# Next batch's input norm, u projection, convolution and x projection inside the current pass; z gates one chunk at a time between scans

## The reference, cut to what matters

```python
# 1 Mamba: DIN 512, 16 states, conv of 4 taps
xn = layer_norm(x, ln_g, ln_b);  u, z = split(xn @ W_in.T)
u  = silu(conv4(u) + conv_b)                    # causal, per channel
dt_in, B, C = split(u @ W_x.T)                  # 16 + 16 + 16
dt = softplus(dt_in @ W_dt.T + dt_bias)
h  = exp(dt * A) * h + dt * B * u               # scan over 512 tokens, each (channel, state)
y  = (sum_n h * C + u * D) * silu(z);  x = LN(x + (x + y @ W_out.T))
# 2 slots: x are the slots, ctx (64 rows) the inputs; three rounds, each needs the one before
for _ in range(3):
    a = softmax over slots of rmsnorm(x) @ Wq.T @ (Pn @ Wk.T).T;  a = a / (column sum + eps)
    slots = gru_cell(a @ (Pn @ Wv.T), slots)
x = LN(x + slots)
# 3 FFN: relu(x @ W_fc.T)**2 @ W_proj.T, then five spike steps, their count over 5;  x = LN(x + that)
```

## Time and profile before

| what | value |
|---|---|
| median of 3 runs | 1797.66 us (1795.49 to 1797.7) |
| profiled execution, its own time | 1799.8 us |
| span of the profiled execution | 1797.8 us |
| busy, share of the span | PE 76%, DVE 76%, ACT 55%, POOL 50% |
| mean granted TensorE clock | 0.858 |
| chain that ended last, by engine | DVE 36%, PE 35%, ACT 11%, issue 7%, POOL 7%, DMA 2% |

### The profile page before, as it was taken

How to read it: one execution, slowest core, us unless ns; L and a number is a source line. 1 busy time by engine, 2 the same in 40 slices (tenths; PEclk the granted TensorE clock), 3 DMA queues, 4 the chain that set the end, 5 groups by cost and what they waited for, 6 DMA issues and landing times.

```text
span 1797.8 us, 16320 instructions
## 1 busy us (share of the span) xinstructions
PE 1359.0 (76%) x5472; PEld 818.6 (46%) x5472; DVE 1370.9 (76%) x1509; ACT 984.8 (55%) x1519; POOL 896.8 (50%) x459
## 2 busy tenths in 40 slices
PE   5455867777788769886788768887688868977965
PEld 2344444453456335463356345563355434553433
DVE  3898488956888798868888698868888798863142
ACT  3542566538663756638464666727474566633532
POOL 0665067723775176623676076733676065741120
PEclk9565978888899879998799979998799978997988
DMA  5632153206231343206331344205332153300000
GB/s 178 247 130 94 51 210 118 105 26 209 108 119 46 131 153 118 94 26 211 105 117 58 105 148 134 106 23 201 105 117 70 60 188 127 117 13 12 0 7 18
DMA packets 64762, 188.89 MB, mean 105 GB/s; under 512 B 6224, under 2 KB 22480, under 8 KB 64720
## 3 DMA queue, kind: packets, MB, share of 16 engines
q1 hardware_dynamic: 64720, 188.37, 30.3%
HBM read 183.62 MB, written 4.72 MB: 105 GB/s over the span
## 4 chain that ended last, share of the span: by engine, by line
DVE 36%; PE 35%; ACT 11%; issue 7%; POOL 7%; DMA 2%; DVEq 0%; ACTq 0%; POOLq 0%; SPq 0%; another core or an unknown queue 0%
DVE reg_a L1081 19%; DVE pb L1072 9%; PE pc L632 5%; POOL reg_a L444 4%; PE pb L487 4%; PE py L646 4%; PE pb L606 3%; PE pc L624 3%; PE px L550 3%; PE px L528 2%; DVE reg_m L930 2%; DMA x_out<-reg_m 2%; PE pb L588 2%; DVE u L1045 1%; ACT reg_a L876 1%
## 5 line engine op out<-in xcount | busy, mean ns | idle before, releaser
L444 POOL TENSOR_TENSOR reg_a<-reg_a,cb 128x1024 f32<-128x1024 f32 x256 | 607.4, 2379 | 304.4 <-DVE reg_a L1081 304.4
L1081 DVE TENSOR_TENSOR_SCAN reg_a<-reg_a,pb 128x1024 f32<-128x1024 f32 x256 | 584.6, 2284 | 34.9 <-ACT reg_a L876 24.8
L646 PE MATMUL py<-ident,reg_a 128*128 128x128 f32 x2048 | 326.4, 314 | 84.5 <-POOL reg_a L444 84.5
L876 ACT ACTIVATE reg_a<-dt,neg_a 128x511 f32<-128x511 f32 x512 | 331.8, 710 | 102.0 <-DVE reg_a L1081 101.2
L646 PEld LDWEIGHTS py<-ident,reg_a 128*128 128x128 f32 x2048 | 280.2, 163 | 183.2 <-POOL reg_a L444 120.2
L1072 DVE TENSOR_TENSOR pb<-bb,pb 128x1024 f32<-128x1024 f32 x256 | 314.7, 1229 | 30.0 <-ACT reg_y L836 2.6
L624 PE MATMUL pc<-x2T,w_fc 128*128 128x512 f32 x224 | 119.0, 658 | 27.1 <-DVE reg_y L1098 20.2
L550 PE MATMUL px<-hT,whh 128*128 128x512 f32 x288 | 137.6, 614 | 0.4 <-ACT xs L779 0.4
L406 POOL TENSOR_TENSOR xs<-xs,hT 128x1024 f32<-128x1024 f32 x24 | 56.7, 2361 | 162.7 <-ACT xs L787 162.7
L632 PE MATMUL pc<-w_pr,reg_m 128*128 128x256 f32 x448 | 111.3, 399 | 8.0 <-ACT y_sb L799 4.1
L565 PE MATMUL pb<-ex,vw 64*128 64x512 f32 x48 | 41.7, 964 | 85.1 <-DVE px L997 85.1
(11 more groups left out here) (174 smaller groups left out, 2265.7 us busy)
## 6 DMA issues: line engine op xcount, KB each, us to landing
bb<-bc_rows SPq DMA_DIRECT2D x256, 512.0 KB, 3.6
cb<-bc_rows SPq DMA_DIRECT2D x64, 512.0 KB, 6.0
xin<-x_in SPq DMA_DIRECT2D x9, 512.0 KB, 3.6
xs<-x_in SPq DMA_DIRECT2D x8, 512.0 KB, 3.5
x_out<-reg_m SPq DMA_DIRECT2D x8, 512.0 KB, 3.4
w_in<-w_inT_in SPq DMA_DIRECT2D x1, 1024.0 KB, 7.1
w_fc<-w_fcT_in SPq DMA_DIRECT2D x1, 1024.0 KB, 10.9
w_pr<-w_prT_in SPq DMA_DIRECT2D x1, 1024.0 KB, 13.2
```

The source lines that it names most:

```text
L444: pool.tensor_tensor(h[:, g % HR], h[:, g % HR], cb[:, 2 * q:2 * q + 2], ALU.mult).then_inc(s["hc_done"], 1)
L646: mm = pe.matmul(py[:, cols_], h[:, g % HR, j, cols_], ident[:], is_transpose=True, start=(q == 0 and j == 0 and i2 == 0), stop=(q == PAIR ...
L876: ins = act.activation(d_a[:, g % DR, j, 1:], dt[:, c, 1:], ACT.Exp, scale=neg_a[:, c * NS + n + j:c * NS + n + j + 1])
L1081: dve.tensor_tensor_scan(h2[:, g % HR], d_a2[:, g % DR], pb[:, 1:3, :].rearrange("p a t -> p (a t)"), 0.0, ALU.mult, ALU.add).then_inc(s[" ...
```

## The change

Four things, taken together.

- The input norm, u projection, convolution, u gate and x projection of batch i+1 are made in pass i (those of batch 0 in the set-up). Convolution steps read the projection straight from PSUM; `upad`, its zeroing and one of the two copies go. The B and C rows are written to DRAM before the barrier, so a pass begins with the dt projection, and SP begins with the x load and the broadcast reads; the context load comes after the read for group 4.
- The z gates are four "zed" steps at slots 3, 4, 7 and 8: projection into `pc`, tanh, gate; each projection waits for the gate of the chunk before it.
- Each engine has its own list of steps; DVE has positions between its scan and the next `mul` ("mid"). Rounds start at slots 0, 10 and 20. The units stand at slots 9, 11 to 17, 19, 20, 22 to 25, 27, 28. `final` 0 stands at slot 30, ahead of the last scan.
- The normalisations of the next input and of the output go from DVE to ACT (scale and shift per row; DVE makes the shift). Softplus of chunks 2 and 3, and the context copies, come after the first decays on ACT.

```diff
+        def place(position, *steps, on=ENGINES):
...
+            for position, *steps in ((b + 1, ("norm", k), ("gate_h", k, 0)), (b + 4, ("colsum", k), ("gate_h", k, 1), ("spread", k)),
+                                     (b + 5, ("gate_x", k, 0), ("gate_x", k, 1), ("gate_h", k, 2)),
+                                     (b + 6, ("gate_h", k, 3), ("gate_x", k, 2), ("gate_x", k, 3), ("cand_h", k, 0)), (b + 7, ("cand_h", k, 1)),
+                                     (b + 8, ("cand_x", k, 0), ("cand_x", k, 1))):
+                place(position, *steps, on=("pe",))
+            for position, *steps in ((b, ("sq", k)), (b + 1, ("norm", k)), (b + 3, ("weigh", k)), (b + 5, ("gate_x", k, 0), ("gate_x", k, 1), ("reset", k)),
+                                     (b + 6, ("gate_x", k, 2), ("gate_x", k, 3)), (b + 7, ("keep", k)), (b + 8, ("cand", k))):
+                place(position, *steps, on=("act",))
+            for position, step in ((("mid", b + 2), ("score", k)), (("mid", b + 3), ("soft", k)), (b + 3, ("recol", k)), (("mid", b + 4), ("renorm", k)),
+                                   (("mid", b + 7), ("hold", k))):
+                place(position, step, on=("dve",))
+            for position, step in ((b + 6, ("keep", k)), (b + 7, ("cand", k))):
+                place(position, step, on=("pool",))
...
+        place(0, ("ctx", 2), ("ctx", 3), ("rest",), on=("act",))
+        place(1, ("sp_exp",), on=("act",))
+        place(2, ("sp_ln",), on=("act",))
+        place(4, ("out_stats",))
+        place(6, ("out_shift",), on=("dve",))
+        place(8, ("out_norm",), on=("act",))
...
+        for position, (half, name, j) in zip(UNITS_AT, units):
             place(position, (name, half, j))
+        for c, position in enumerate(GATES_AT):
+            place(position, ("zed", c))
+        for n, b in enumerate(ROUNDS_AT):
+            place_round(n, b)
...
+        place(23, ("next_stats",))
+        place(25, ("next_shift",), on=("dve",))
+        place(26, ("next_norm",), on=("act",))
+        place(29, ("turn",), on=("pe", "act"))
+        place(30, ("final", 0), on=("pe", "dve"))
+        place(31, ("u", 0), ("u", 1), on=("pe", "act"))
+        place(31, ("conv", 0), on=("dve",))
+        place(33, ("final", 1), on=("pool",))
+        place(34, ("u", 2), on=("pe",))
+        place(34, ("uth", 0), ("uth", 1), ("u", 2), on=("act",))
+        place("end", ("final", 1), ("ugate", 0), ("ugate", 1), ("conv", 2), ("ugate", 2), ("ugate", 3), on=("dve",))
+        place("end", ("u", 3), on=("pe",))
+        place("end", ("u", 3), ("final", 3), ("uth", 2), ("uth", 3), on=("act",))
+        place("late", ("final", 2), on=("pe",))
...
             def z_proj(c):
+                if c:
+                    pe.wait_ge(s["sz_ready"], c)
+                else:
+                    pe.wait_ge(s["sp_abs"], 2)
                 for e in range(ET):
-                    mm = pe.matmul(z_banks[c], w_in[:, e, (DT + c) * P:(DT + c + 1) * P], xnT[:, e], start=(e == 0), stop=(e == ET - 1))
+                    mm = pe.matmul(pc[:], w_in[:, e, (DT + c) * P:(DT + c + 1) * P], xnT[:, e], start=(e == 0), stop=(e == ET - 1))
...
+            def shifted(name, src, dst):
+                act.wait_ge(s[f"{name}_shift"], 1)
+                for i2 in range(TT):
+                    act.activation(dst[:, i2], src[:, i2], ACT.Identity, scale=stats[name][3][:, i2:i2 + 1],
+                                   bias=shift[name][:, i2:i2 + 1]).then_inc(s[f"{name}_norm"], 1)
...
+                filler("end")
                 if mamba:
                     pe.wait_ge(s["scan_done"], GROUPS)
                     pe.wait_ge(s["yz_done"], DT - 1)
                     for c in range(DT - 1):
                         out_proj(c)
-                filler("end")
+                filler("late")
                 if mamba:
                     pe.wait_ge(s["yz_done"], DT)
                     out_proj(DT - 1)
-                if mamba:
-                    next_transposes()
-                    pe.wait_ge(s["res_done"], TT)
-                    u_proj(0)
-                    u_proj(1)
+                    x_proj()
                     pe.wait_ge(s["post_norm"], TT)
```

More of the change, by code:

```diff
@@ L171, in decoder_layer @@
                      sb(f"{n}_rstd", [P, TT])) for n in ("next", "post", "x2", "out")}
+        shift = {n: sb(f"{n}_sh", [P, TT]) for n in ("next", "out")}
         pb = ps("pb", [P, 4, L])
@@ L251, in decoder_layer @@
         plan = {}
[L253 to L264, removed]
@@ new lines, in decoder_layer @@
+        place("start", ("ctx", 0), ("spike", 0), ("ctx_norm",))
+        place("head", ("ctx", 1), ("ctx", 2), ("ctx", 3), on=("pe",))
+        place("head", ("ctx", 1), on=("act",))
+        for n in range(1, SPIKE_OPS):
+            place("head", ("spike", n), on=("dve",))
+        place(0, ("ctx", 2), ("ctx", 3), ("rest",), on=("act",))
[3 more added lines that the diff above has]
+        place(6, ("out_shift",), on=("dve",))
@@ L304, in reads_before_slot, with take @@
             return sum(step[0] == "up" or (step[0] == "down" and step[2] % 2 == 1)
-                       for position in range(g) for step in plan.get(position, ()))
+                       for position in range(g) for step in plan.get(("pe", position), ()))
         def chunks_back(g):
             return sum(chunk_end(position) is not None for position in range(g + 1))
-        def take(position, slot_step, mamba, slots, ffn, spikes):
-            for step in plan.get(position, ()):
+        def take(engine, position, slot_step, mamba, slots, ffn, spikes):
+            for step in plan.get((engine, position), ()):
                 kind = step[0]
@@ L738, in _, with u_start @@
-            next_copies()
-            act.wait_ge(s["upad_zero"], 1)
-            for j in range(DT):
-                u_copies(j)
-            meet(act, 1)
-            def slot_step(step, k=0, j=0, back=0, ffn=False, spikes=False, mamba=False):
+                    act.activation(xnT[:, e], px[:, e, :], ACT.Identity, scale=col("ln_g", e), bias=col("ln_b", e)).then_inc(s["xnT_ready"], 1)
+            def u_start(c):
+                act.wait_ge(s["u_full"], c + 1)
+                act.activation(u2[:, c], u_banks[c], ACT.Identity, scale=col("conv_w", c * KC + KC - 1),
+                               bias=col("conv_b", c)).then_inc(s["uacc_ready"], 1)
@@ new lines, in _, with softplus_parts @@
+            for c in (0, 1):
+                u_start(c)
+            u_tanh(0)
+            u_tanh(1)
+            u_start(2)
+            u_start(3)
+            u_tanh(2)
+            u_tanh(3)
+            keep_bc()
+            meet(act, 1)
+            def softplus_parts(c):
+                act.wait_ge(s["pre_full"], 1 + c)
+                act.activation(dt[:, c], dt_banks[c], ACT.Relu, bias=col("dt_bias", c))
+                act.activation(sp[:, c], dt_banks[c], ACT.Abs, bias=col("dt_bias", c)).then_inc(s["sp_abs"], 1)
@@ L745, in slot_step @@
+            def slot_step(step, k=0, j=0, back=0, ffn=False, spikes=False, mamba=False, slots=False):
+                if step == "rest":
+                    softplus_parts(2)
+                    softplus_parts(3)
+                    return
                 if step == "ctx":
```

347 lines of the change are left out of this document (173 added, 174 removed).

## The result

The changed kernel takes 1867.5 us (median of four runs, 1866.4 to 1868.5) against 1797.7 before: a ratio of 1.039, 95% interval 1.037 to 1.041. The forecast was 1824, range 1765 to 1860: the sign is right, the loss is 70 us instead of 26.

What follows compares the result with a forecast made beforehand. Three rounds in turn, not the scans or a full engine, were taken to bound a pass. Passes 3 to 7 +20.5, pass 2 +9, pass 1 -8, pass 0 +4, last three +1: +26.5 on 1799.8, forecast 1824 us, range 1765 to 1860.

Steps and rivals of the forecast that it cites:

- The sign: Whole kernel: the change makes it slower, given a chance of 0.67, against 0.26 for faster and 0.07 for the same.
- the rounds and not the scans are the string: Full pass: three rounds in turn hold it, so a shorter head helps only if rounds end earlier; ends near 70, 121, 174.
- Rival (a): Full pass: the scans set its length, not the rounds; 185 us a pass, about 1680 in all; chance 0.10.
- the convolution is hidden: Tail: the convolution, 12 x 0.67 us on DVE, lies beside the u and output projections and adds nothing.
- One reading of the prediction: ACT table load between norm and soft: 1.28 us with the next activation right behind; the skill's drain would give 1831 in all.
- I take 209, nearer the high bound: Full pass, passes 3 to 7: sum of 203 to 212 us, taken as 209, +4.1 each and +20.5 together.
- The low clock: PE behind idle stretches: norm and two z projections take 1.9 or 3.7 us each; idle stretches of 4 to 5 us.
- The units in rounds 1 and 2: FFN units on PE inside the rounds: round 1 takes 50.2 to 50.8 us, round 2 51.7 to 53.6.
- The way from round 2 to `final` 0: End of a pass: C product 2.4, hsum 1.0, transposes 0.9 before `final` 0; last scan ends 10 to 11 after round 2.
- The last three: +1: The last three passes, which have rounds but no scans: together 1 us longer.
- pass 1: Pass 1, without FFN units: DVE sets the pace in rounds 1 and 2; 187 us against 195.0, -8.
- Rival (c): Hand-overs between engines: each costs a little more than rows show; 3 us more a pass, 1849 to 1875; chance 0.10.

Runs made afterwards that it cites:

- run 1: Changed kernel with each slot's round steps ahead of its z gate, units still ahead of both: 1813.6 us, 1.009 of the kernel before.
- run 2: Changed kernel with each slot's round steps ahead of both its FFN units and its z gates: 1786.5 us, 0.994 of the kernel before.
- run 3: Changed kernel with all FFN units at the slots of the kernel before, order inside a slot unchanged: 1836.1 us, 1.021 of the kernel before.
- run 4: Changed kernel with `final` 0 one slot later, behind scan 31 instead of ahead of it: 1854.1 us, 1.030 of the kernel before.
- run 7: Changed kernel with norm's first product and gate_h 1 each computed twice more in PE's idle time of round 0: 1847.5 us, 1.028 of the kernel before.
- run 15: Changed kernel with only the second FFN half at the slots of the kernel before: 1845.6 us, 1.027 of the kernel before.
- run 11: Changed kernel with each convolution step on 8 columns instead of 509 to 511, giving another output: 1865.1 us, 1.036 of the kernel before.
- run 16: Changed kernel with two 128x512 copies added at the end of ACT's list in each pass with a scan: 1894.8 us, 1.054 of the kernel before.
- run 17: Changed kernel with four 128x512 copies added at the end of ACT's list in each pass with a scan: 1898.0 us, 1.056 of the kernel before.
- run 18: Kernel before with two copies added at the end of ACT's list in each pass with a scan: 1816.6 us, 1.011 of the kernel before.
- run 9: Changed kernel with the edits of run 2 and run 4, tanh pair ahead of x2T copies, x2 transposes behind the last output projection: 1759.5 us, 0.978.
- run 13: Run 9 with the FFN units at the slots of the kernel before in the last three passes alone: 1753.1 us, 0.976 of the kernel before.
- run 8: Kernel before with each slot's round steps ahead of its FFN units, nothing else changed: 1779.9 us, 0.991 of the kernel before.
- run 10: Changed kernel with the edits of run 2 and run 4, and norm's first product computed twice more: 1772.5 us, 0.984 of the kernel before.
- run 12: Run 9 with norm's first product computed twice more, and old unit slots in the last three passes alone: 1759.0 us, 0.977 of the kernel before.

## Why the prediction was right or wrong

*Right.* The sign, and the mechanism: the rounds and not the scans are the string, the chain of steps that sets the pass. In the changed kernel and runs 1 to 4, 7 and 15 a full pass ends 36 to 39.5 after its third round, wherever that lies, and run 1, which only puts the z gates behind the round steps of their slots, takes 54 us off. Rival (a), 1680 us, is out. The rounds end 69.6, 121.5 and 175.6 into a full pass (forecast 70, 121 and 174). The first scan came at 11.2 (forecast 10.1), soft at 28.4 (27.9 to 30.3), scan 4 at 35.5 (33.0 to 37.3), hold of round 1 waits for PE, PE runs at the half clock behind its idle stretches, and the convolution is hidden (run 11).

One reading of the prediction needs a better row: behind the table load of the earlier trace rows ACT waits 2.56 for PE, so that row can't show what stands right behind a load. Others do. In the kernel before a load of 1.28 starts at 841.32 and the next activation at 842.61; in the changed kernel one starts at 1054.53, ahead of the first tanh of z, and the next activation at 1055.82. The Trainium skill, page ScalarE: Activation LUTs, section What ACT_TABLE_LOAD costs, adds a drain of about 1.38 to each switch. The traces show none in these places.

*Wrong: the size of a full pass, "I take 209, nearer the high bound"* (+4.1 a pass; it was +10.2). On the profiled execution +26.5 was forecast and 67.7 came; of the 41 between them 27 lie in passes 3 to 7, 9 in the last three and 5 in passes 0 to 2. Part by part, bounds and measured: round 0 63.9 to 70.1, 69.6; round 1 50.2 to 50.8, 51.9; round 2 51.7 to 53.6, 54.1; last scan behind round 2 10 to 11, 11.6; tail 26.6, 27.8. Round 0 stands near its upper bound, the other four 0.5 to 1.2 over theirs, and the pass of 215.0 is 3 over the top of the sum, 212. Three terms were mis-sized, by the rows:
- The low clock. The high bound has 3.7 for norm and for each of two z projections, and the high clock for the steps behind them. From the start of the second z projection to the end of gate_h 1 that would make 6.6 (3.7, 1.0 and 1.9); it took 8.1 at a granted clock of 0.58, and renorm waited 1.69 for it. In the tail the bounds have 3.6 for u projections of chunks 2 and 3 together; the first of them alone took 3.25 instead of 1.88. Run 7 gives 3.4 a pass back by keeping the clock up in round 0, some of which the sum had.
- The units in rounds 1 and 2 (1.6 over the bounds together). They were summed by PE's work. ACT's two activations for each unit (0.60 and 0.63) stand ahead of norm and weigh as well: score and soft of these rounds wait 15.2 for ACT, against 5.7 in the kernel before, and runs 2 and 15 gain there.
- The way from round 2 to `final` 0. The sum had 4.3 for it (C product, hsum, transposes); `final` 0 starts 6.1 after the end of round 2, having waited 2.45 for PE, and scan 31 stands behind it. Run 4 takes scan 31 out of that and 3.4 off the pass.

A further cause is argued, not shown: if lengths of a full pass come in steps (runs 16 to 18), 209 was hardly to be had, the neighbours being 208.1 and 211.6, and up to 3.4 a pass lies in that. How the miss divides between all these, the runs don't settle.

*Wrong: "The last three: +1."* This was never worked out from rows; +9.7 came. The units were followed through the full pass and not through the pass that has rounds but no scans. Old slots there, and only there, give 8.9 back (runs 9 and 13).

*Wrong, and partly cancelling by luck:* pass 1 gained 2, not 8 (without z gates ahead it gains 5.8, run 1), pass 2 lost 13, not 9 (it is the first with units, and 18.2 longer than pass 1; 3.2 before), pass 0 gained 1 instead of losing 4. Rival (c), 3 us more a pass, has the measured time in its range. Whether hand-overs between engines cost more than the rows show, which is the reason it gave, no run here tests.

## What to carry to other kernels

In in-order queues a filler is not free because its engine has room: what counts is which step of the chained string stands behind it and what the filler itself waits for; put the string's steps first in each slot, then look for places. When work moves into a pass, follow it through every kind of pass that runs it, fills and drains too. In round 0 here the chain pays for PE's idle time twice, once as the wait and once as the slower matmuls behind it; filling that time paid in one order (run 7) and not in another (runs 10 and 12). And before a gain is put down to a change, give the kernel before the same new order (run 8).

## What was not expected of the hardware

After 4 to 5 us idle four matmuls of 128x512 took 2.96 to 3.78 us instead of 1.88, some or all of that at 1.2 GHz, and added, useless matmuls in the idle time made the kernel 1% faster (run 7), but cost 6 us in another order (runs 12 and 13). Most full passes took lengths about 3.4 us apart, in the kernel before as well; 1.15 us of added work cost 3.4. The rows show that the granted clock changes at other places of a shifted pass; what makes the lengths fall on steps, no run here shows.
